# First scan: 160 of each direction's 1024 state columns computed on GpSimd

## What is computed

```
xn      = layernorm(x) * ln_w + ln_b
x_ssm, gate = split(xn @ in_proj_w)            # 256 channels each
A       = -clip(exp(A_log), -10, -0.01)        # [256, 16]
step:   h = clip(h * A + x_t[:, :, None] * B, -10, 10)    # h is [32, 256, 16]
        y = sum over the 16 states of h * C
out     = (scan forward + scan backward) * 0.5 * silu(gate)
return  out @ out_proj_w
```

## Time and profile before

| | us |
|---|---|
| median of 3 runs | 1285.28 |
| lowest and highest run | 1284.97, 1285.29 |
| the profiled execution | 1284.66 |
| its span | 1282.9 |
| VectorE busy in the span | 1021.1 |
| TensorE busy in the span | 1032.4 |
| GpSimd busy in the span | 557.6 |

### The profile page before, as it was taken

One profiled execution on the slowest core, in us unless ns is written; L12 is line 12 of the kernel. 1 busy time (PEld: TensorE's weight loads), 2 busy tenths in 40 slices (PEclk: granted clock), 3 DMA queues, 4 the chain that ended last, 5 costly groups with the idle time before them and its releaser, 6 DMA issues. The chain is left out here.

```text
span 1282.9 us, 22875 instructions
## 1 busy us (share of the span) xinstructions
PE 1032.4 (80%) x8295; PEld 739.7 (58%) x8295; DVE 1021.1 (80%) x2091; ACT 699.0 (54%) x1468; POOL 557.6 (43%) x870
## 2 busy tenths in 40 slices
PE   2899887457599999999998797572888888767696
PEld 1556544144599999999997656220333333535555
DVE  4699999765698889889974559649999999667565
ACT  2867544025466666666663162543666666147453
POOL 3100000002798888888873140100777777214351
PEclk9999799778799999999999799666899999879989
DMA  1000000011301111121100000001000000000001
GB/s 43 1 1 2 2 1 1 1 46 64 129 36 68 70 73 73 73 74 67 56 2 1 21 3 1 1 1 48 16 1 1 1 1 1 1 1 3 2 1 30
DMA packets 16849, 32.49 MB, mean 25 GB/s; under 512 B 5072, under 2 KB 11968, under 8 KB 16736
## 3 DMA queue, kind: packets, MB, share of 16 engines
q1 hardware_dynamic: 16736, 31.02, 7.0%
HBM read 30.10 MB, written 0.92 MB: 24 GB/s over the span
## 5 line engine op out<-in xcount | busy, mean ns | idle before, releaser
L2021 POOL TENSOR_TENSOR m_h_in<-m_dtu,m_bs 128x448 f32<-128x448 f32 x128 | 144.7, 1134 | 114.8 <-DVE m_dtu L2054 69.3
L2075 DVE TENSOR_TENSOR_SCAN m_hs<-msp_da,m_h_in 128x448 f32<-128x448 f32 x128 | 137.3, 1073 | 2.9 <-ACT msp_da L2043 1.6
L672 DVE SCALAR_TENSOR_TENSOR l0r_u<-l0r_u,l0r_a_col 128x1024 f32<-128x1024 f32 x110 | 135.7, 1273 | 0.0
L1054 POOL TENSOR_TENSOR bl_sc<-bl_sc,bl_topall 125x1456 f32<-125x1456 f32 x32 | 105.3, 3290 | 58.9 <-ACT bl_topall L1216 58.9
L627 ACT ACTIVATE l0r_u<-l0rp_pu 128x512 f32<-128x512 f32 x224 | 111.5, 648 | 33.6 <-PE l0rp_pu L563 33.6
L1993 PE MATMUL msp_py<-m_hc,ident 128*128 128x448 f32 x256 | 119.1, 548 | 0.0
L2034 ACT ACTIVATE m_bs<-msp_pb 128x448 f32<-128x448 f32 x128 | 69.6, 544 | 79.5 <-PE msp_pb L1977 79.4
L563 PE MATMUL l0rp_pu<-l0r_xs,l0r_eb 32*128 32x256 f32 x896 | 102.2, 419 | 4.8 <-ACT l0r_u L627 4.1
L1291 PE MATMUL bl_pS<-b_qw,bl_xcT 128*125 128x112 f32 x768 | 104.0, 278 | 0.0
L766 POOL MEMSET bq_lT<- 128x256 f32 x1 | 0.3, 311 | 236.0 <-POOLq L107 236.0
L1223 ACT ACTIVATE bl_sq<-bl_pX 125x512 f32<-125x512 f32 x96 | 57.2, 597 | 63.0 <-PE bl_pX L1280 34.5
(11 more groups left out here) (396 smaller groups left out, 2484.8 us busy)
## 6 DMA issues: line engine op xcount, KB each, us to landing
b_xc<-in_ctx SPq DMA_DIRECT2D x16, 750.0 KB
bl_more<-in_ctx SPq DMA_DIRECT2D x16, 750.0 KB
x_tm<-in_x SPq DMA_DIRECT2D x1, 896.0 KB, 5.7
cw_cT<-in_ctx_headT SPq DMA_DIRECT2D x1, 896.0 KB
out_dram<-x_tm SPq DMA_DIRECT2D x4, 224.0 KB, 2.5
w_up<-in_L_ffn_w SPq DMA_DIRECT2D x1, 512.0 KB, 4.0
w_down<-in_L_ffn_w SPq DMA_DIRECT2D x1, 512.0 KB, 5.2
l0s_win<-in_L_attn_in_proj_wT SPq DMA_DIRECT2D x1, 256.0 KB, 2.5
```

What stands on the lines that cost most here:

```text
L672: ve.scalar_tensor_tensor(state(c, i, r), prev, a_col[:, :], state(c, i, r), ALU.mult, ALU.add).then_inc(step_done, 1)
L1054: pool.tensor_tensor(sc[0:KP, n % 3, :, :], sc[0:KP, n % 3, :, :], over(topall[0:KP, n % 2, :].unsqueeze(1), [KP, KT + 1, QR]), ALU.subtra ...
L2021: pool.tensor_tensor(h_in[:, n % NU, :], dtu[:, half, cols], bs[:, n % NU, :], ALU.mult).then_inc(s["db"], 1)
L2075: ve.tensor_tensor_scan(hs[:, n % NU, :], da[:, n % 2, 0:CH], h_in[:, n % NU, :], 0.0, ALU.mult, ALU.add).then_inc(s["scan"], 1)
```

## The change

GpSimd takes the last 5 of the 32 groups, columns 864 to 1023 (OWN = 864), of both directions. VectorE's decays and clips cover columns 0 to 863. GpSimd's access pattern `states(c, i)` picks the forward slot and the backward slot of a step as one operand of 2 x 160 columns. A step on GpSimd is a multiply by `a_col` into the new tile `decayed`, an add into `u`, and the clip; each waits on `pool_step` for the one before. GpSimd waits for the same fills as VectorE. TensorE's `sums(c)` now also waits for GpSimd's last clip of the chunk, and ScalarE's `fill(c)` for GpSimd's first step of chunk c - 2. VectorE waits for nothing of GpSimd's.

```diff
--- before.py
+++ after.py
@@ -415,6 +415,7 @@
 NCH = L // TC
 RC = 3
 W = NG * B
+OWN = W - 5 * B
 
 
 def pair_of_chunks(c):
@@ -450,6 +451,7 @@
         cA = sb2("cA", [P, 2, NG])
         mine = sb2("mine", [P, CPG])
         a_col = sb2("a_col", [P, 1])
+        decayed = sb2("decayed", [P, 2, W - OWN])
         with nc.Block() as block:
             @block.sync
             def _(sp):
@@ -472,6 +474,7 @@
             built, turned, got, spreads = (core.sem(f"l0r_{s}") for s in ("built", "turned", "got", "spreads"))
             made_cexp = core.sem("l0r_cexp")
             step_done, u_made, filled = (core.sem(f"l0r_{s}") for s in ("step", "u_made", "filled"))
+            pool_step = core.sem("l0r_pool_step")
             y_made, y_taken, y_gated = (core.sem(f"l0r_{s}") for s in ("y_made", "y_taken", "y_gated"))
             x_made, x_kept = core.sem("l0r_x_made"), core.sem("l0r_x_kept")
             with nc.Block() as block:
@@ -566,6 +569,7 @@
 
                     def sums(c):
                         pe.wait_ge(step_done, scanned(c * TC + TC - 1))
+                        pe.wait_ge(pool_step, 3 * (c * TC + TC - 1) + 1)
                         if c == 0:
                             pe.wait_ge(made_cexp, 1)
                             pe.wait_ge(x_kept, 16)
@@ -606,6 +610,24 @@
                         last = pool.tensor_scalar(cexp[:, g, at:at + CPG], mine[:, :], cA[:, 0, g:g + 1], None, ALU.mult)
                     last.then_inc(made_cexp, 1)
 
+                    def states(c, i):
+                        step = 2 * TC - 1 - 4 * i
+                        first, stop = 2 * i, 2 * (TC - i) if step > 0 else 2 * (TC - 1 - i)
+                        return u[:, c % RC].rearrange("p t r x -> p (t r) x")[:, first:stop:step, OWN:W]
+
+                    for c in range(NCH):
+                        pool.wait_ge(filled, (c + 1) * FILLS)
+                        for i in range(TC):
+                            t = c * TC + i
+                            if t:
+                                pool.wait_ge(pool_step, 3 * t - 2)
+                                pool.tensor_scalar(decayed[:, :, :], states(c, i - 1) if i else states(c - 1, TC - 1), a_col[:, :],
+                                                   None, ALU.mult).then_inc(pool_step, 1)
+                                pool.wait_ge(pool_step, 3 * t - 1)
+                                pool.tensor_tensor(states(c, i), states(c, i), decayed[:, :, :], ALU.add).then_inc(pool_step, 1)
+                                pool.wait_ge(pool_step, 3 * t)
+                            pool.tensor_scalar(states(c, i), states(c, i), 10.0, -10.0, ALU.min, ALU.max).then_inc(pool_step, 1)
+
                 @block.scalar
                 def _(act):
                     def keep(k):
@@ -618,6 +640,7 @@
                         if c >= RC:
                             act.wait_ge(y_made, c - RC + 1)
                             act.wait_ge(step_done, scanned((c - RC + 1) * TC))
+                            act.wait_ge(pool_step, 3 * (c - RC + 1) * TC + 1)
                         for w in range(WAVES):
                             half, j0 = wave(w)
                             for gl in range(4):
@@ -648,7 +671,7 @@
                 @block.vector
                 def _(ve):
                     def state(c, i, r):
-                        return u[:, c % RC, TC - 1 - i if r else i, r, :]
+                        return u[:, c % RC, TC - 1 - i if r else i, r, 0:OWN]
 
                     def gated(c):
                         ve.wait_ge(y_made, c + 1)
```

## The result

| | before | after |
|---|---|---|
| median of 4 runs | 1285.28 us | 1311.90 us |
| lowest and highest | 1284.97, 1285.38 | 1310.57, 1314.11 |
| span of the profiled execution | 1282.9 us | 1312.3 us |

The ratio is 1.0209, 95% interval 1.0192 to 1.0227: 27 us slower (25 to 29). The forecast was 50 us slower, 1335, with a range of 1306 to 1365. The direction and the main mechanism held, and about half of the size.

The account below looks back on a forecast made before the run. VectorE bounds the first scan. Streams 149.4, GpSimd's turns 97.9, fixed parts 5.6 and gating 5.5, of which 4 come back, make 254.4 against 204.6 us: +50 on 1284.66, forecast 1335 us, range 1306 to 1365.

Parts of the forecast that it names:

- main case: First scan: both engines take turns as they come; +50 us, 1335 us, bounds 1313 to 1364; turn-taking 82%.
- rival B: First scan: VectorE's decays are not blocked by GpSimd, its clips are; 1307 us, chance 5%.
- What bounds the kernel, and the saving: First scan: VectorE is the bound; 160 fewer columns cut a step from 3.60 to 3.10 us, saving 27 us.
- The blocking: First scan: each GpSimd instruction takes its duration less 0.13 us out of VectorE's time; 97.9 us of turns.
- Rival A: First scan: the engines don't block each other, under 0.17 us of VectorE per GpSimd instruction; 1259 us, chance 7%.
- Rival C: First scan: VectorE, always ready, keeps the way until it must stop for a fill; 1389 us, chance 6%.
- The price of the add: GpSimd's add over 320 columns in the scan: 0.86 us long, a turn of 0.73 us.
- The price of the clip: GpSimd's clip over 320 columns in the scan: 0.60 us long, a turn of 0.47 us.
- The price of the multiply: GpSimd's multiply by a column over 320 columns in the scan: 0.70 us long, a turn of 0.57 us.
- 4 us come back at the gating: VectorE's 12 gating instructions have an input in PSUM, so GpSimd works beneath; of 5.5 us, 4 come back.
- Running ahead: Scan: GpSimd gets four turns a step, needs three, so runs ahead to the filled chunks' end; pool_step waits cost nothing.

Follow-up runs that it names:

- single kernels: Changed kernel with only one of GpSimd's three instructions left per step, its columns otherwise not scanned: add 1289.74 us, multiply 1268.75, clip 1268.41.
- the kernel with the constant: Changed kernel with GpSimd's multiply taking the constant -0.5 in place of the column a_col: 1317.26 us, ratio 1.0263 to the kernel before.

## Why the prediction was right, and where its numbers were not

The mechanism was right, and two of its prices, the clip's and the multiply's, were not. That the time fell into the range is in part luck. The main case's own lower bound was 1313 us; the median, 1311.90, is 1 us below it, and lies in the range only because this reached down to rival B, which did not happen.

**What bounds the kernel, and the saving.** Right: a step without GpSimd is 3.10 us, 177.2 us of work for 204.5.

**The blocking.** Right that it is the main term and turns a gain of 27 us into a loss; by single kernels, the three instructions together take 35.5 + 13.9 + 12.6 = 62 us of VectorE, in the changed kernel 57 (234.1 less 177.2), where the prediction had 254.4 less 177.2 = 77. Rival A falls: a lone add, at 0.63 us, costs 3.7 times the 0.17 at which A began. Rival B falls with the decay of 1.72 us. Rival C falls for the kernel as a whole: VectorE stopped for no fill, and GpSimd's last clip ended at 275.6, before VectorE's at 276.5. Its premise, that VectorE can pass a GpSimd instruction that was there first, did show: for the multiply in each step, and for an add or a clip now and then in their own kernels.

**The price of the add.** Right: 0.86 us alone, 0.61 of VectorE.

**The price of the clip.** Right in kind, wrong in size: 0.454 us and not 0.60, 0.22 us of VectorE and not 0.37 (0.47 less the fixed part that it hides). The slope of 1.11 ns a column, drawn from a line with one operation to one with two, both with column operands, was too steep for constants. That is 8 of the 20 us too much (77 less 57). The Trainium skill (GPSIMD Engine Reference, Elementwise — side-by-side cycle accounting), from whose 769 ns for 512 elements I had an estimate of 0.48 us, was nearer; for the multiply it was further off than I was.

**The price of the multiply.** The step that failed: "a GpSimd instruction takes its duration less 0.13 us out of VectorE's time". It was read from tensor_tensor alone and carried over to tensor_scalar with one operation. That one lasts 1.085 us and takes 0.25 of VectorE (in the full kernel it stretches a decay by 0.19); I had 0.70 and, less what it hides, 0.47. The two errors, a duration too short and a share too large, partly cancelled; had I used L1820's row with the rule, the forecast would have been further off. That is 12 us too much. With the clip's 8 this is all of the 20. The prediction also let 4 us come back at the gating; against them stand the 5 us by which the three together (57) take less than alone (62). Of these 5, the step above shows 3 in the multiply, which takes 0.19 us there and not 0.25; the rest no run takes apart.

**Running ahead.** Wrong: GpSimd did not get ahead. The multiply loses its turn to VectorE's second clip, and three turns a step are left; with the constant it keeps this turn, but then the add waits through the first decay, and three are left again. It cost nothing, for VectorE waits for GpSimd nowhere and the table of waits has 0.5 us of ScalarE's for GpSimd and nothing of TensorE's.

**Rival A's time.** Had the engines not blocked each other, the gain would have been some 16 to 19 us (by ratio and by medians) and not 26. VectorE's gaps of 9.4 us show why: 4.4 are the start, for which I had given 1, and 5.0 are TensorE's loop, 13.4 us at a granted clock of 0.75 (126.19 to 139.59). I had the 11.8 of the earlier trace rows alone, where the clock was 0.93.

Open: what decides whether a waiting GpSimd instruction is passed by VectorE. That reading its column first makes the multiply ask too late fits the kernel with the constant but is not shown by itself; it does not explain the 3.42 us shown above, nor the add of 2.77 us and the clip of 2.18 us, which read no column. Why a one-operation tensor_scalar holds the shared way so little was not tried either.

## What to carry to other kernels

Before work is split between VectorE and GpSimd, price it in time taken from VectorE, not by whether GpSimd's own chain fits beside: with both operands in SBUF a tensor_tensor on GpSimd took 0.63 of its 0.86 us out of VectorE's time, and all three cost VectorE 3.3 ns a column (1.05 us for 320) to save it 1.56. Measure each form of GpSimd instruction by itself, since three of one size here took 0.63, 0.25 and 0.22 us. A rule read from one form is only a guess for another.

## What the runs showed of the hardware

On GpSimd a tensor_scalar with one operation takes 2.5 ns a column and with two 0.8 (1007 and 454 ns at 320 columns, with constants; a column operand adds to it, 1085 ns for the first). A second, neutral operation made the multiply shorter, 766 ns at its shortest beside VectorE for 1326. An add of 864 ns held a VectorE decay up by 0.61 us, a one-operation multiply of 1085 ns by 0.19. GpSimd's memset of 320 columns leaves VectorE's two-input instructions at their 1.11 us.
